# Attention and channel-mix block on 8 cores: the spare tile's LayerNorm steps one head pair earlier, and the output stores on GpSimd's queue

## What is computed

```python
def _layernorm(x): return (x - mean(x)) / sqrt(var(x) + 1e-5)

def attn(x):                       # 16 heads, scale 1/8 on the scores
    x = layernorm(x) * gamma + beta
    q, k, v = x @ Wq, x @ Wk, x @ Wv
    w = softmax(q @ k.T / 8)
    return (w @ v) @ Wo

def ffn(x):                        # x_prev is x shifted by one token
    xr = mu_r * x + (1 - mu_r) * x_prev
    xk = mu_k * x + (1 - mu_k) * x_prev
    r = sigmoid(xr @ W_r.T)
    return r * (square(relu(xk @ W_k.T)) @ W_v.T)

x = x + _layernorm(attn(_layernorm(x)))
x = x + _layernorm(ffn(_layernorm(x)))
```

## Time and profile before

| | us |
|---|---|
| runs of this kernel | 3738.64, 3824.22, 3827.25 (median 3824.22) |
| the profiled execution | 3740.24 |
| its span on the slowest core (core 3) | 3738.7 |
| spans of the eight cores | 3716.9 to 3738.7 |

### The profile page before, as it was taken

How to read it: one execution, slowest core, us unless ns; L and a number is a source line. 1 busy time by engine, 2 the same in 40 slices (tenths; PEclk the granted TensorE clock), 3 DMA queues, 4 the chain that set the end, 5 groups by cost and what they waited for, 6 DMA issues and landing times.

```text
span 3738.7 us, 38316 instructions; the slowest of 8 cores (3716.9 to 3738.7 us)
## 1 busy us (share of the span) xinstructions
PE 2977.8 (80%) x12322; PEld 928.2 (25%) x12322; DVE 1317.9 (35%) x1826; ACT 2480.0 (66%) x2803; POOL 107.7 (3%) x201
## 2 busy tenths in 40 slices
PE   0199998998988988889889889889889871576675
PEld 0034432222222222222222222222222220232232
DVE  3544442222332232332242232332322332546454
ACT  3422228998897888889788878888878860242434
POOL 1000000000000000000000000000000001000000
PEclk9899999999999999999999999999999985888897
DMA  8611111000001001010100010000010016142231
GB/s 201 165 32 46 47 42 26 9 5 26 30 18 41 21 23 36 23 32 13 37 28 22 29 33 23 28 30 23 22 37 20 18 54 121 32 112 58 75 95 68
DMA packets 138462, 168.22 MB, mean 45 GB/s; under 512 B 77840, under 2 KB 102416, under 8 KB 138272
## 3 DMA queue, kind: packets, MB, share of 16 engines
q1 hardware_dynamic: 110976, 92.31, 9.9%
q0 software_dynamic: 22688, 65.07, 6.6%
q10 hardware_dynamic: 4608, 8.39, 0.6%
HBM read 96.49 MB, written 67.14 MB: 44 GB/s over the span
## 4 chain that ended last, share of the span: by engine, by line
PE 61%; DVE 19%; issue 6%; ACT 4%; SPq 4%; DMA 3%; DVEq 2%; ACTq 1%; POOL 0%; POOLq 0%
PE ps_o L854 24%; PE ps_sc L788 17%; DVE stage L911 10%; PE ps_sc L423 6%; PE ps_w L631 4%; SPq L1058 3%; PE ps_sc L467 3%; DVEq L44 2%; PE ps_bcj L922 2%; PE ps_o L881 2%; DMA wk_sb<-wk 1%; DVE stage L893 1%; DVE xrT_sb L1089 1%; DVE xkT_sb L1095 1%; PE ps_k L1145 1%
## 5 line engine op out<-in xcount | busy, mean ns | idle before, releaser
L866 ACT ACTIVATE exp_sb<-ps_sc,bias_cols 128x1024 bf16<-128x1024 f32 x2048 | 2084.4, 1167 | 345.5 <-PE ps_sc L788 327.3
L854 PE MATMUL ps_o<-exp_sb,v_sb 128*65 128x512 bf16 x3840 | 1228.2, 402 | 17.9 <-DVE stage L893 17.9
L788 PE MATMUL ps_sc<-qtc_sb,kT_sb 64*128 64x512 bf16 x4096 | 824.8, 393 | 138.6 <-ACT exp_sb L866 37.4
L893 DVE COPY stage<-ps_o 65x512 f32<-65x512 f32 x128 | 82.2, 682 | 1505.1 <-PE ps_o L881 1505.1
L788 PEld LDWEIGHTS ps_sc<-qtc_sb,kT_sb 64*128 64x128 bf16 x4096 | 243.0, 93 | 1070.4 <-issue 1070.4
L854 PEld LDWEIGHTS ps_o<-exp_sb,v_sb 128*65 128x65 bf16 x3840 | 275.7, 111 | 499.4 <-issue 496.7
L911 DVE RECIPROCAL stage<-stage 1x512 f32<-1x512 f32 x112 | 367.1, 3315 | 5.1
L1117 PE MATMUL ps_wo<-wrt_sb,xrT_sb 128*128 128x512 bf16 x512 | 136.0, 427 | 151.5 <-DVE xkT_sb L1098 85.4
L631 PE MATMUL ps_w<-wo_sb,at_sb 128*128 128x512 bf16 x512 | 179.0, 513 | 89.4 <-DVE wo_sb L639 81.2
L435 ACT ACTIVATE qstage<-ps_sc,bqk_sb 128x512 bf16<-128x512 f32 x64 | 44.0, 687 | 218.4 <-PE ps_sc L423 218.4
L1179 PE MATMUL ps_wo<-wvt_sb,kact_sb 128*128 128x512 bf16 x512 | 127.1, 412 | 74.1 <-DVE gg_sb L1209 61.7
(11 more groups left out here) (115 smaller groups left out, 1610.3 us busy)
## 6 DMA issues: line engine op xcount, KB each, us to landing
x_sb<-x SPq DMA_DIRECT2D x64, 512.0 KB, 4.7
x_h<-x1r_sb POOLq DMA_DIRECT2D x32, 512.0 KB, 3.6
x1c_sb<-x_h POOLq DMA_DIRECT2D x8, 2048.0 KB, 16.0
out<-ob_sb SPq DMA_DIRECT2D x8, 2048.0 KB, 10.3
xa_h<-xa_sb ACTq DMA_DIRECT2D x32, 256.0 KB, 4.9
qt_h<-qstage POOLq DMA_DIRECT2D x64, 128.0 KB, 2.2
qtc_sb<-qt_h SPq DMA_DIRECT2D x16, 512.0 KB, 4.2
attn_h<-attnb SPq DMA_DIRECT2D x128, 64.0 KB, 2.1
```

The lines of the kernel that those rows point to most:

```text
L788: e.matmul(ps_sc[:, (bp + r2) * 512:(bp + r2 + 1) * 512], kT_sb[lo:lo + 64, pj * S + kt * 128: pj * S + (kt + 1) * 128], qtc_sb[lo:lo + 64 ...
L854: e.matmul(ps_o[r2][0:65, :], v_sb[:, ktg * HW + hh * 65: ktg * HW + hh * 65 + 65], exp_sb[:, eo + r2 * 512: eo + r2 * 512 + 512], start=s ...
L866: e.activation(exp_sb[:, eo:eo + 1024], ps_sc[:, bp * 512:(bp + 2) * 512], AF.Exp, bias=bias_cols[:, pj:pj + 1], scale=0.125),
L893: e.tensor_copy(stage_sb[si][0:65, :], ps_o[r2][0:65, :]), inc=s_aev)
```

## The change

It has two parts. In the attention stage the four remaining steps of the spare tile `e3` move by one pair: `As` and `Bv` from pair 1 to pair 0, `Bs` and `C` from pair 2 to pair 1, there ahead of `stepT(t0)`. In the channel mix the wait for the last add and the store of the finished chunk go from SP's list to POOL's. The matmuls and their order stay.

```diff
@@ -806,17 +806,17 @@
                                 if pj == 0:
+                                    if qc >= 2:
+                                        p3a_As(e3)
+                                        p3a_Bv(e3)
                                     p3a_loads(qc - 1)
                                 elif pj == 1:
                                     if qc >= 2:
-                                        p3a_As(e3)
-                                        p3a_Bv(e3)
+                                        p3a_Bs(e3)
+                                        p3a_C(e3)
                                     p3a_stepT(t0)
                                 elif pj in (2, 4, 6):
                                     k = pj // 2 - 1
-                                    if k == 0 and qc >= 2:
-                                        p3a_Bs(e3)
-                                        p3a_C(e3)
                                     p3a_As(t0 + k)
                                     p3a_Bv(t0 + k)
@@ -1259,8 +1259,8 @@
-            ph.wait("sync", s_v, out_done[ch])
-            ph.op("sync", lambda e, pp=pp, ch=ch:
+            ph.wait("gpsimd", s_v, out_done[ch])
+            ph.op("gpsimd", lambda e, pp=pp, ch=ch:
                   e.dma_start(out=out_h[ch * 512:(ch + 1) * 512, :].rearrange("(i p) d -> p i d", p=128),
```

## The result

The changed kernel is faster by more than was forecast: its ratio to the kernel before is 0.9855, 95% interval 0.9835 to 0.9876, against 3708.1 / 3740.2 = 0.991 in the forecast. That is under the 2% that the prediction called the resolution of a measurement, but the interval excludes both 1 and 0.991. The profiled execution took 3691.4 us (before 3740.2), with 3689.9 us on its slowest core, now core 6, and a mean span over the cores of 3682.5 us (before 3727.4). Some runs of either kernel take 2 to 3.5% longer with a lower clock on one die (the median of before's first three was such a run); they are left out of the comparisons.

The account below looks back on a forecast made before the run. It took woven steps stretching attention pairs (PE waiting for DVE's copy in pair 1) and DVE's transpose waits as the loss: 3740.2 - 28.9 + 3.6 - 7.2 + 0.4 = 3708.1 us; own range 3688 to 3725, whole range up to 3800.

Parts of the forecast that it names:

- the low end of its own range: 3687.7 us: no cost in pair 0 or the last store, pair 5 drawn to pair 3's length (16.4 us less).
- Pairs 1 and 2, 28.9 us: Attention, query chunks 2 to 7: pair 1 saves 3.23 us, pair 2 1.59, by matching pairs 3 and 4; 28.9 in all.
- the prediction's signs: If right: pairs 1 and 2 near 75.8 us, copy L639 waiting for PE, pair 0 one 0.5 us break, no later transpose waits.
- Pairs 3 and 5, held fixed: Attention stage: the forecast gave these pairs no gain, keeping 40.54 and 43.27 us; only the range's low end shortened pair 5.
- Pair 0, 3.6 us: Attention, six query chunks: gaining As and Bv costs pair 0 0.60 us each (0 to 1.50), 3.6 us in all.
- the rule that the prediction cited from the Trainium skill: A matmul stream interrupted every round returns to the throttled clock; pair 0 would cost its upper end, 5.4 us more in all.
- The transposes, 7.2 us: Channel mix: issued without waiting behind the store, they remove DVE's five waits after chunk 0; 7.2 us saved, lower end 0.
- the last store, 0.4 us: End of span: POOL issues the store in 0.75 us, SP in 0.38; 0.4 us more, ends 0 and 4 us.
- The further 0.4 us of the Trainium skill: Last store: first byte after about 1 us from GpSimd against 0.6 us from SyncE, 0.4 us more; not in the sum.
- Pair 1 at the slow pace: Rival, attention stage: pair 1 becomes like pair 5, pair 0 costs its upper end; 3729.9 us; chance 0.20.
- no gain from the transposes: Rival, channel mix: DVE waits as long for ACT or PE instead; 3715.3 us; chance 0.12.
- the slower case: Rival: pair 0's break lowers PE's pace, both projections run at 43.3 us; 3746.3 us; chance 0.04.

Follow-up runs that it names:

- e3: Kernel before, with DVE copying the first Wo group in pair 1 ahead of the rest of Bv, all steps left in their pairs; ratio 0.9896 to before.
- e5: Changed kernel with four more unused statistics on DVE ahead of the Wo copies in pair 1, putting PE's wait back; ratio 0.9964 to before.
- e6: Kernel before with only As and Bv of the spare tile moved to pair 0, Bs and C left in pair 2; ratio 0.9923 to before.
- e1: Kernel before with only the channel mix stores moved from SP to POOL; ratio 0.9988 to before.
- e4: Kernel before with two more unused 128x1 ACT instructions at step 8 of pair 0, adding only the break; ratio 1.001 to before.
- e12: Changed kernel with two more unused statistics on DVE ahead of the Wo copies in pair 1; profiled execution 3709.4 us, no interval.
- e10: Changed kernel with the second Wo group of pairs 1, 3 and 5 sent at step 12 instead of step 8; ratio 0.9673 to before.

## Why the prediction was right and where it was wrong

The direction was right and the time of the profiled execution, 3691.4 us, lies in the range, 17 us under the forecast and 3 us above the low end of its own range (3688 to 3725). The terms missed in both directions. For six chunks, forecast and mean over the cores: pairs 1 and 2 28.9 and 32.5 us gained; pairs 3 and 5 nothing and 12.1; pairs 0 and 7 3.6 and 5.4 lost; the transposes 7.2 and 7.8 gained; the last store 0.4 and 2.8 lost. That is 32.1 us forecast and 44.2 measured, of 44.9 us in the mean span. The other 4 us of the miss are in the slowest core, which lies 11.3 us above the mean span before and 7.4 after.

*Pairs 1 and 2, 28.9 us.* The mechanism was right for pair 1: DVE's work ahead of the copy made PE wait, and e3 shows that this alone carries 5.71 us of a chunk. The size was wrong in the step "Pair 1 now holds Bs(e3), C(e3) and a stepT, which is word for word what pair 3 holds. So it should take pair 3's 40.54 us". Pair 3's length was not that of its instructions alone; it had an echo of pair 1's wait in it (3.41 us for its first group, in before as in e5, 1.90 without the wait). Pair 1 came to 39.36 us. Pairs 1 and 2 gave 4.92 + 0.50 = 5.42 us on the mean for the 3.23 + 1.59 = 4.82 forecast, so the near match is partly luck: pair 1 was put too low and pair 2 too high. For pair 2 the mechanism was wrong as well. The prediction took the 1.59 us for the price of the second pair of columns, but with both pairs of columns left in it, it takes 35.49 us in e3 and 35.48 in e6; its 36.89 on core 3 was the lower clock (0.91 against 0.95 in pair 4). Of the prediction's signs, pairs 1 and 2 together take 74.8 us on core 6 (39.25 + 35.52; 75.8 foretold), and that the copy L639 would wait for PE did not come.

*Pairs 3 and 5, held fixed.* That is the larger part of the miss: on the mean they gave 2.01 us for each chunk, 12 us in all, of some 14 us by which the attention stage gained more than forecast (39.3 for 28.9 - 3.6). On core 3, whose pair 5 stood at 43.27 in chunks 3 to 7, pair 5 alone gave 4.0 us in each of these. The low end of the range had held this possibility (pair 5 drawn along), but with pair 3's 40.54 as its floor, and the text said that no row told why pair 5 was longer: the two slow groups in it, and the granted clock of 0.88, were in the same trace.

*Pair 0, 3.6 us.* Forecast 0.60, measured 0.29, and 0.61 more in pair 7, whose lengths stand at 35.2 us (granted clock 1.00) or 37.8 (0.91). The break itself is 0.48 us, and where pair 0 has the same mean clock in both kernels it goes from 44.9 to 45.4 us, so 0.60 was near. By the rule that the prediction cited from the Trainium skill (TensorE: Matmul & The Clock Gate, "HAM oscillation — how this bites in real kernels") pair 0 would have paid 1.50: that did not come. The case in that section of the Trainium skill is a wait longer than the burst of matmuls ahead of it, and a break of half a microsecond is none. In pair 1 the trace agrees with the rule, a wait of 4.48 us behind 8 matmuls of 1.90 us and then 3.27 us for what takes 1.89, so it was set against the wrong gap. Pair 5 before, with 3.57 us behind a wait of 0.94, is a case that it does not cover.

*The transposes, 7.2 us, and the last store, 0.4 us.* The stage lost 7.8 us on the mean, all five waits went. The store at the end cost 2.8 us instead of 0.4: the sum took the issue (0.37 us longer, as measured) but for the time behind it a value where the two queues are alike; it was inside the bounds (0 to 4 us). The store lands 9.1 us after its issue on core 6 (3680.8 to 3689.9; before 6.7), so the sign of being wrong that the prediction had named, over 7 us, did come, for this term. The further 0.4 us of the Trainium skill (DMA: Bandwidth & Descriptors, "Specifications") would not have closed it either; where the 2.4 us behind the issue go was not taken apart.

*The rivals.* Pair 1 at the slow pace, no gain from the transposes, and the slower case are all excluded by the rows above.

*Open.* Pair 5 is at 40.4 to 41.0 us in before, e1, e3 and e6 and at 39.4 to 39.9 in after, e4, e5 and e12, that is sometimes with and sometimes without the break in pair 0, the doubled columns in pair 2 and the wait in pair 1. The shortest length (under 39.7 us) stands in 24, 28, 18 and 21 of the 48 places of the first four kernels and in 46, 44, 41 and 40 of the last four. All of the last four have the break in pair 0, but so has e6. None of the three orders these runs by itself. So of the 2.01 us that pairs 3 and 5 gave, the 0.79 of pair 3 are shown to come from the wait in pair 1; the cause of the 1.22 of pair 5 is not shown. Why the clock falls at one place and not at another with the same instructions, and why pairs 2, 4 and 6 stay at the upper level in e10, was not taken apart either.

## What to carry to other kernels

Before you take a neighbour's length as the price of a moved step, look at the granted clock of the neighbour: two stretches with the same instructions and two lengths are the sign. A wait of PE behind one short copy in another engine's list can be worth more than it lasts (here 3.1 us in the pair for 1.7 us of waiting), and the cure is the order there (copy first, the rest behind) or other matmuls in between, which here gained 1.8% on top of the change's 1.45%. A store with a wait ahead of loads in one list wants to be behind them, not in another queue; and what ends the span should be small and on the faster queue.

## What was not expected of the hardware

- After a wait of PE of 3.01 us the next 8 matmuls of 128x512 took 3.14 us instead of 1.89; after one of 1.35 us they did not. After 4.54 us they took 3.57 us, and a group some 74 us later 3.41 us. A short wait is no guarantee: before, 13 of 48 second groups in pair 5 took 3.57 us behind 0.94 us.
- With the two Wo groups four steps apart (e10) in place of one interruption, the granted clock is 1.00 in the pair after as well (0.95 in the changed kernel), worth 0.9 to 1.3 us in each.
- The same instructions give a few fixed pair lengths, each with its mean granted clock: 39.2 us at 1.00, 40.5 at 0.96, 43.3 at 0.88.
- The issue of 8 transposes takes 10.0 to 10.4 us alone (chunks 2 to 7 of the changed kernel, cores 3 and 6) and 16.5 to 21.8 us where a 2 MB store and a 2 MB load are issued with them (before, the same cores). Which of the two slows it was not tested.
- A 2 MB store as the last work ends 9.6 us after the last add through POOL and 6.8 us through SP; four stores of 512 KB, each behind its own add, end 3.0 us after it.
